# Two accumulations in two PSUM banks taken in turn, in cross-attention and in a recurrent state product

## The chip, the cores and the metric

The kernel runs on one core of a Trainium2 chip. Its time is the device time of one execution in microseconds (us); the number given for a kernel is the median of its runs. Times inside an execution come from the trace of one profiled execution.

## What is computed

A decoder layer over 16 batches of 224 rows of 512 features, in fp32, in three sublayers, each followed by a residual addition and a layer norm:

```python
x = layernorm(x + self_attention(x))              # 16 heads, causal
x = layernorm(x + cross_attention(x, ctx_1024))   # one head, 750 rows of context per batch
x = layernorm(x + ffn(x))                         # a recurrence over the 16 batches

# cross-attention
q = x @ Wq.T + bq;  k = ctx @ Wk.T + bk;  v = ctx @ Wv.T + bv
attended = softmax(q @ k.T) @ v

# ffn: c is a state [224, 512], xt is one batch [224, 512], 16 steps
ft = sigmoid(xt @ wf.T + c @ uf.T + bf)
it = sigmoid(xt @ wi.T + c @ ui.T + bi)
gt = tanh(xt @ wc.T + c @ uc.T + bc)
c  = ft * c + it * gt
h  = tanh(x @ wo.T + c_final @ uo.T + bo)
```

## The kernel before

Four stages follow one another: self-attention, cross-attention (from about 410 to 900 us of the span), the recurrence (to about 1420) and the output gate with the last norm. Each engine has its own instruction stream, written out by hand; the engines meet through semaphores, and an instruction behind a wait stays behind it. Nothing reorders the matmuls: their order is that of the Python loops in the function of TensorE.

**Split operands.** An fp32 product is made of three: each operand is split into a rounded part (hi, type fp32r) and the rest (lo), and hi x hi, lo x hi and hi x lo are added up in PSUM. KC = 4 chunks of 128 of the 512 features are contracted, XC = 6 chunks of 125 of the 750 rows of context. So an accumulation has 12 matmuls (3 products x 4 chunks) or 18 (3 x 6). Each matmul comes with its own load of the stationary operand; in the trace the loads have a row of their own (PEld), which runs ahead of the matmuls.

**Cross-attention, TensorE's turn for a batch** (function step). With T = 224 rows in TC = 2 halves of R = 112:
- p_turn turns the softmax numerators of the batch before (12 transposes, L786).
- zt (L797): the query side multiplied by a folded matrix m, 512 features out. Four results of 128 x 224 lie two to a bank in the two banks of ps_h: results 0 and 1 in the first, 2 and 3 in the second (function pair). One result is completed after the other, 12 matmuls each.
- ot (L810): context times turned weights, for the batch before. Again four results of 128 x 224, two to a bank of ps_g, 18 matmuls each, one after the other.
- s (L824): the scores, 112 rows by two halves of 376 columns. The two halves lie in two banks, and the loop over them is the innermost, with the same stationary operand for both. This one is not changed.
- x1_turn turns the next batch's rows (L778).
- out (L836): the result of ot times the value weights, for the batch before: 112 rows by 512 columns, once for each half of the rows, each in a bank of ps_h, 12 matmuls each, one half after the other.

zt waits for both residuals of the batch before last (r_done), because out leaves its results in the banks that zt writes. The residual (L989, DVE) reads a half of the rows of out once out_done says that this half is complete, and out_done is raised once for each half. DVE's stream for a batch holds, in this order at its end: the maxima of the scores, x1tl (L939, L940), the two residuals, the reciprocal of the sums. POOL's x1b (L1057) waits for the residuals as well.

**Recurrence.** c_gate makes one gate for one half of the features: two tiles of 128 x 448 in two banks of ps_gate. For each tile c_tile takes four matmuls of 448 columns (hi weights times the state's hi and lo, side by side, L1274) and then four of 224 (lo weights times the state's hi, L1276). gate_done is raised once after both tiles. There are 6 gates in each of 15 steps. Between them stands x_part (L1255): the input's share of the gates, tiles of 128 x 448 of 12 matmuls, alternating between two banks from tile to tile, not from matmul to matmul.

Of the kernel before, what the change touches and what calls it, by code (L numbers as in the profile page):

```python
# [20 lines left out]
B, T, D = 16, 224, 512  # L21
H, C = 16, 32
TC = 2
R = T // TC
KC = D // 128
TX = 750
XC, XR = 6, 125
# [7 lines left out]
def wait(eng, sem, value):  # L35

    if not (isinstance(value, int) and value <= 0):
        eng.wait_ge(sem, value)


def within(n, end):
    return not isinstance(n, int) or 0 <= n < end
# [602 lines left out]
def cross_attention(nc, io, x1, x2, raw, raw_in, shared):  # L645
# [5 lines left out]
    with ExitStack() as ctx:  # L651
        def sb(name, shape, dt=F32):
            return ctx.enter_context(nc.sbuf_tensor("x_" + name, shape, dt))

        def sem(name):
            return ctx.enter_context(nc.semaphore("x_" + name))

        identity, bv_all = shared.identity, shared.bv_all
        m_hi, m_lo, wv_hi, wv_lo = shared.m_hi, shared.m_lo, shared.wv_hi, shared.wv_lo
# [24 lines left out]
        ot_hi = sb("ot_hi", [128, KC, T], F32R)  # L684
        ot_lo = sb("ot_lo", [128, KC, T], F32R)
# [8 lines left out]
        ps_g = ctx.enter_context(nc.psum_tensor("x_ps_g", [128, 2, 512], F32))  # L694
        ps_h = ctx.enter_context(nc.psum_tensor("x_ps_h", [128, 2, 512], F32))
# [28 lines left out]
        out_done = sem("out_done")  # L724
# [10 lines left out]
        def pair(bank, k):  # L735

            return bank[:, k // 2, (k % 2) * T:(k % 2) * T + T]
# [30 lines left out]
        @block.tensor  # L768
        def _(pe):

            pe.wait_ge(pad_done, 2)

            def x1_turn(b):
                wait(pe, x1_in, 16 * (b + 1))
                wait(pe, otl_done, b - 1)
                for k in range(KC):
                    for c in range(TC):
                        mm = pe.transpose(ps_g[:, k // 2, (k % 2) * T + c * R:(k % 2) * T + c * R + R],  # L778
                                          x1_raw[:, c, 128 * k:128 * k + 128], identity[0:R, 0:R])
                mm.then_inc(x1t_done, 1)  # L780

            def p_turn(b):
                wait(pe, exp_done, TC * (b + 1))
                for j in range(XC):
                    for c in range(TC):
                        mm = pe.transpose(ps_s[0:XR, j // 2, (j % 2) * T + c * R:(j % 2) * T + c * R + R],  # L786
                                          p[:, c, XR * j:XR * j + XR], identity[0:R, 0:R])
                mm.then_inc(pt_done, 1)

            def zt(b):  # L790
                wait(pe, x1tl_done, b + 1)
                wait(pe, r_done, TC * (b - 1))
                for ck in range(KC):
                    i = 0
                    for m, x in ((m_hi, x1t_hi), (m_lo, x1t_hi), (m_hi, x1t_lo)):
                        for k in range(KC):
                            mm = pe.matmul(pair(ps_h, ck), m[:, k, 128 * ck:128 * ck + 128], x[:, k, :],  # L797
                                           start=(i == 0), stop=(i == 3 * KC - 1))
                            i += 1
                mm.then_inc(zt_done, 1)  # L800

            def ot(b):
                wait(pe, ptl_done, b + 1)
                wait(pe, cxl_done, XC * (b + 1))
                wait(pe, x1tl_done, min(b + 2, B) if isinstance(b, int) else b + 2)
                for dk in range(KC):
                    i = 0
                    for v, q in ((cx_hi, pt_hi), (cx_lo, pt_hi), (cx_hi, pt_lo)):
                        for j in range(XC):
                            mm = pe.matmul(pair(ps_g, dk), v[:, j, 128 * dk:128 * dk + 128], q[:, j, :],  # L810
                                           start=(i == 0), stop=(i == 3 * XC - 1))
                            i += 1
                mm.then_inc(ot_done, 1)

            def s(b):
                wait(pe, ztl_done, b + 1)
                wait(pe, ctl_done, KC * (b + 1))
                wait(pe, ptl_done, b)
                for c in range(TC):
                    i = 0  # L820
                    for z, x in ((zt_hi, ct_hi), (zt_hi, ct_lo), (zt_lo, ct_hi)):
                        for k in range(KC):
                            for half in range(2):
                                mm = pe.matmul(ps_s[0:R, 2 * c + half, 0:XH + 1], z[:, k, c * R:c * R + R],  # L824
                                               x[:, k, half * XH:half * XH + XH + 1], start=(i == 0), stop=(i == 3 * KC - 1))
                            i += 1
                    mm.then_inc(s_done, 1)

            def out(b):
                wait(pe, otl_done, b + 1)  # L830
                wait(pe, ztl_done, min(b + 2, B) if isinstance(b, int) else b + 2)
                for c in range(TC):
                    i = 0
                    for y, w in ((ot_hi, wv_hi), (ot_hi, wv_lo), (ot_lo, wv_hi)):
                        for k in range(KC):
                            mm = pe.matmul(ps_h[0:R, c, :], y[:, k, c * R:c * R + R], w[:, k, :],  # L836
                                           start=(i == 0), stop=(i == 3 * KC - 1))
                            i += 1
                    mm.then_inc(out_done, 1)

            def step(b):
                if within(b - 1, B):
                    p_turn(b - 1)
                if within(b, B):
                    zt(b)
                if within(b - 1, B):
                    ot(b - 1)
                if within(b, B):
                    s(b)
                if within(b + 1, B):  # L850
                    x1_turn(b + 1)
                if within(b - 1, B):
                    out(b - 1)

            x1_turn(0)
            for b in range(2):
                step(b)
            with pe.Fori(2, B - 1) as b:
                step(b)
            step(B - 1)  # L860
            step(B)
# [247 lines left out]
def recurrence(nc, io, x2, identity, cc, wf, wi, raw, raw_in):  # L1109

    GATES = ("f", "i", "c")
    HC = KC // 2
    TILES = 3 * KC
    with ExitStack() as ctx:
# [6 lines left out]
        w = {"wf": wf, "wi": wi}  # L1121
# [16 lines left out]
        ps_gate = ctx.enter_context(nc.psum_tensor("f_ps_gate", [128, 6, 512], F32))  # L1138
# [67 lines left out]
        @block.gpsimd  # L1206
        def _(pool):
            pool.memset(state[:], 0.0).then_inc(made, 1)

            def split(i):  # L1210
                _, hi, lo = plan[i]
                pool.wait_ge(raw_in[i % 3], 16 * (i // 3 + 2))
                pool.tensor_copy(hi[:], raw[i % 3][:]).then_inc(w_rounded[i], 1)  # L1213
                pool.wait_ge(w_rounded[i], 1)
                pool.tensor_tensor(lo[:], raw[i % 3][:], hi[:], ALU.subtract).then_inc(w_split[i], 1)

            split(1)
            split(4)
            pool.wait_ge(xpart_done, TILES * (B // 2))
            split(6)  # L1220
            split(7)

        @block.tensor
        def _(pe):
# [42 lines left out]
                                           start=(k == 0), stop=(k == KC - 1))  # L1267
                mm.then_inc(u_done, 1)

            def c_tile(half, j, k2, ks):  # L1270
                m = slice(128 * (HC * half + k2), 128 * (HC * half + k2) + 128)
                hi, lo = w["u" + GATES[j]]
                for k in ks:
                    pe.matmul(ps_gate[:, 2 * j + k2, 0:2 * T], hi[:, k, m], cc[:, k, :, :], start=(k == 0), stop=False, skip_group_check=True)  # L1274
                for k in ks:
                    mm = pe.matmul(ps_gate[:, 2 * j + k2, 0:T], lo[:, k, m], cc[:, k, 0, :], start=False, stop=(k == KC - 1),  # L1276
                                   skip_group_check=True)
                return mm

            def c_gate(b, half, j, ks=range(KC)):  # L1280
                if ks[0] == 0:
                    if isinstance(b, int) and b == 1 and half == 0:
                        pe.wait_ge(w_split[3 + j], 1)
                        pe.wait_ge(u_bias_done, 3)
                    wait(pe, add_done, 6 * (b - 1) + 3 * half + j - 2)
                for k2 in range(HC):
                    mm = c_tile(half, j, k2, ks)
                if ks[-1] == KC - 1:
                    mm.then_inc(gate_done, 1)

# [551 lines left out]
```

## Time and profile before

| | |
|---|---|
| median of 3 runs | 1537.86 us (1536.14 to 1540.71) |
| profiled execution | 1533.36 us |
| its span | 1531.6 us |
| mean granted TensorE clock | 0.972 |
| TensorE matmul, share of the span | 95% |
| weight loads (PEld) | 82% |
| DVE / ACT / POOL | 59% / 42% / 36% |

The span is the time from the first to the last instruction of the program in the profiled execution. A share is the time in which the engine had an instruction running; matmuls overlap, so a busy TensorE is not one at its peak. L797 is line 797 of the kernel. A clock of 1.00 is 2.4 GHz, 0.50 is 1.2 GHz.

### The profile page before, as it was taken

Reading aid. Unit: us, or ns where it says so; the run is one execution under the profiler, and the core shown is the slowest. Engines: PE = TensorE matmul, PEld = TensorE weight load, DVE = VectorE, ACT = ScalarE, POOL = GpSimd, SP = SyncE. Lnnn points to the kernel's source line nnn. Section 1 sums busy time; section 2 is a strip of 40 time slices with the busy share of each in tenths; the row PEclk is TensorE's granted clock in tenths of the full one; section 3 lists DMA queues with packets and bytes.
Section 4 is the critical chain, followed back from the end, with each engine's and each line's share of the span. In section 5 each row is a group of like instructions: output and inputs, shape, how many; then the busy total and the mean of one; then the engine's idle time right before and its main releaser. Section 6 shows DMA issues by size and latency. Waiting matters only on the chain. (4 is left out here: it accounts for less than half of the span.)

```text
span 1531.6 us, 28869 instructions
## 1 busy us (share of the span) xinstructions
PE 1455.9 (95%) x10322; PEld 1262.1 (82%) x10322; DVE 902.2 (59%) x1995; ACT 638.9 (42%) x1887; POOL 554.3 (36%) x430
## 2 busy tenths in 40 slices
PE   7999999999699999999999959999999999999897
PEld 3677777776498999999999849999999999998685
DVE  4578888887445665665665532253445435546587
ACT  4477777776243444434434313222222222221232
POOL 2445555554365656656566421000000000003254
PEclk9899999999899999999999979899999999999999
DMA  6113232243236343343334122200000000000553
GB/s 187 39 51 97 85 95 73 84 148 91 73 109 196 135 156 122 135 146 131 133 133 150 53 77 78 80 25 1 24 22 2 24 0 24 1 1 0 158 165 118
DMA packets 71605, 131.01 MB, mean 86 GB/s; under 512 B 7218, under 2 KB 15410, under 8 KB 71540
## 3 DMA queue, kind: packets, MB, share of 16 engines
q1 hardware_dynamic: 71540, 130.17, 26.6%
q8 instruction: 37, 0.61, 0.2%
q14 instruction: 28, 0.23, 0.0%
HBM read 106.30 MB, written 22.02 MB: 84 GB/s over the span
## 5 line engine op out<-in xcount | busy, mean ns | idle before, releaser
L401 ACT ACTIVATE a_p<-a_ps_s,a_nmax 112x224 f32<-112x224 f32 (+1 forms) x512 | 198.8, 417 | 96.3 <-DVE a_nmax L467 96.3
L617 POOL TENSOR_TENSOR a_p<-a_p,a_rinv 112x896 f32<-112x896 f32 (+1 forms) x128 | 164.9, 1309 | 171.8 <-DVE a_rinv L475 166.1
L1213 POOL CAST f_wf_hi<-w_raw 128x2048 fp32r<-128x2048 f32 x1 | 1.9, 1894 | 453.2 <-PE f_ps_x L1255 453.2
L1070 POOL TENSOR_TENSOR x_cx_lo<-s_cx_raw,x_cx_hi 125x512 fp32r<-125x512 f32 x96 | 120.8, 1300 | 73.1 <-ACT x_cx_hi L901 73.1
L1443 DVE TENSOR_TENSOR f_gate<-f_ps_gate,f_xg_early 128x448 f32<-128x448 f32 x45 | 28.1, 624 | 197.7 <-PE f_ps_gate L1276 197.7
L1359 ACT ACTIVATE f_gate<-f_gate 128x448 f32<-128x448 f32 x90 | 52.1, 579 | 185.3 <-DVE f_gate L1446 185.3
L1064 POOL TENSOR_TENSOR x_ct_lo<-s_ct_raw,x_ct_hi 128x750 fp32r<-128x750 f32 x64 | 118.7, 1885 | 12.6 <-ACT x_ct_hi L875 12.6
L482 DVE COPY a_pt<-a_ps_t 112x448 f32<-112x448 f32 x128 | 79.3, 620 | 64.2 <-PE a_ps_t L277 64.1
L277 PEld LDWEIGHTS a_ps_t<-identity,a_p 112*112 112x112 f32 x768 | 87.4, 135 | 33.4 <-issue 12.2
L401 ACT ACTIVATION_READ_ACCUMULATOR a_p<-a_ps_s,a_nmax 112x1 f32 x512 | 113.7, 222 | 0.0
L277 PE MATMUL a_ps_t<-identity,a_p 112*112 112x112 f32 x768 | 107.3, 262 | 0.0
L466 DVE TENSOR_REDUCE a_nmax<-a_ps_s 112x1 f32<-112x224 f32 x256 | 97.0, 379 | 12.5 <-PE a_ps_s L264 12.2
L1057 POOL TENSOR_TENSOR x_x1b<-s_x_raw,s_bv_all 112x1024 f32<-112x1024 f32 x16 | 38.1, 2380 | 88.4 <-DVE x_r L989 88.4
L467 DVE TENSOR_REDUCE a_nmax<-a_ps_s 112x1 f32<-112x112 f32 x256 | 67.4, 263 | 0.0
L977 DVE TENSOR_REDUCE x_smax<-x_ps_s 112x1 f32<-112x750 f32 x32 | 30.0, 939 | 58.5 <-PE x_ps_s L824 58.5
L309 PE MATMUL a_ps_w<-a_w_hi,a_yt_lo 128*112 128x512 f32 x128 | 64.3, 516 | 0.0
L1274 PE MATMUL f_ps_gate<-f_cc,f_uf_hi 128*128 128x448 f32 x240 | 59.8, 370 | 3.5 <-DVE f_cc L1470 3.5
L1346 ACT ACTIVATE f_xg_early<-f_ps_x,f_bias 128x448 f32<-128x448 f32 x48 | 30.4, 633 | 72.9 <-PE f_ps_x L1255 72.9
L908 ACT ACTIVATE x_p<-x_ps_s,x_shift 112x750 f32<-112x750 f32 x32 | 28.4, 888 | 75.8 <-DVE x_shift L982 75.8
L1346 ACT ACTIVATE f_xg_late<-f_ps_x,f_bias 128x448 f32<-128x448 f32 x48 | 30.4, 633 | 70.8 <-PE f_ps_x L1255 70.7
L1274 PE MATMUL f_ps_gate<-f_cc,f_ui_hi 128*128 128x448 f32 x240 | 59.8, 370 | 0.0
L1274 PE MATMUL f_ps_gate<-f_cc,f_uc_hi 128*128 128x448 f32 x240 | 59.5, 368 | 0.0
(220 smaller groups left out, 3863.6 us busy)
## 6 DMA issues: line engine op xcount, KB each, us to landing
s_ct_raw<-in_ct SPq DMA_DIRECT2D x16, 1500.0 KB, 7.9
s_cx_raw<-in_cx SPq DMA_DIRECT2D x16, 1500.0 KB
a_xt<-in_xt SPq DMA_DIRECT2D x16, 448.0 KB, 3.9
a_xrow<-in_x SPq DMA_DIRECT2D x16, 448.0 KB, 3.5
a_xres<-in_x SPq DMA_DIRECT2D x16, 448.0 KB, 4.5
x_scratch<-a_xn SPq DMA_DIRECT2D x16, 448.0 KB, 3.1
s_x_raw<-x_scratch SPq DMA_DIRECT2D x16, 448.0 KB, 3.6
x_scratch<-x_xn SPq DMA_DIRECT2D x16, 448.0 KB, 6.2
```

The costliest lines, as they stand in the source:

```text
L277: mm = pe.transpose(ps_t[0:R, (g + unit) % 2, h * R:h * R + R], src, identity[0:R, 0:R])
L309: mm = pe.matmul(ps_w[0:R, :], *products[i], start=(i == 0), stop=(i == len(products) - 1))
L401: e = act.activation((p1 if c else p0)[:, g, h, :], src, ACT.Exp, bias=nmax[:, g % 2, c, h:h + 1], accum_out=rsum[:, g % 2, c, h:h + 1])
L466: dve.tensor_reduce(nmax[:, g % 2, 1, h:h + 1], ps_s[0:R, h, 0:T], AX.X, ALU.max, negate=True)
L467: dve.tensor_reduce(nmax[:, g % 2, 0, h:h + 1], ps_s[0:R, h, T:T + R], AX.X, ALU.max, negate=True)\
L482: dve.tensor_copy(transposed(g, unit), unit_bank(g, unit)).then_inc(ptd_done, 1)
L617: pool.tensor_tensor(p[:, g, :, :], p[:, g, :, :], inv, ALU.mult).then_inc(norm_done, 1)
L1064: pool.tensor_tensor(ct_lo[:, k, 0:TX], ct_raw[:, k, :], ct_hi[:, k, 0:TX], ALU.subtract).then_inc(ctl_done, 1)
L1070: pool.tensor_tensor(cx_lo[:, j, :], cx_raw[:, j, :], cx_hi[:, j, :], ALU.subtract).then_inc(cxl_done, 1)
L1274: pe.matmul(ps_gate[:, 2 * j + k2, 0:2 * T], hi[:, k, m], cc[:, k, :, :], start=(k == 0), stop=False, skip_group_check=True)
L1346: act.activation(pre(odd_pair, half, j)[:, k2, :, :], ps_x[:, t % 2, 0:2 * T].rearrange("p (a t) -> p a t", a=2), ACT.Identity, bias=bias[ ...
L1359: act.activation(gate[:, j, cols, :], gate[:, j, cols, :], ACT.Tanh, scale=0.5 if j < 2 else 1.0).then_inc(act_done, 1)
```

## The change

Three products of cross-attention and the state product of the recurrence are put in another order. The same matmuls are done on the same operands, into the same places.

- zt and ot: results 0 and 2 (in different banks) are accumulated together, one matmul for each in turn, and then results 1 and 3.
- out: both halves of the rows are accumulated together; out_done is still raised for each half, at its last matmul, and these are now the last two.
- c_gate: the two tiles of a gate take turns; all matmuls with hi weights come first, then all with lo weights. The function c_tile is gone.

```diff
-                for ck in range(KC):
+                for first in range(KC // 2):
                     i = 0
                     for m, x in ((m_hi, x1t_hi), (m_lo, x1t_hi), (m_hi, x1t_lo)):
                         for k in range(KC):
-                            mm = pe.matmul(pair(ps_h, ck), m[:, k, 128 * ck:128 * ck + 128], x[:, k, :],
-                                           start=(i == 0), stop=(i == 3 * KC - 1))
+                            for ck in (first, first + KC // 2):
+                                mm = pe.matmul(pair(ps_h, ck), m[:, k, 128 * ck:128 * ck + 128], x[:, k, :],
+                                               start=(i == 0), stop=(i == 3 * KC - 1))
                             i += 1
...
-                for dk in range(KC):
+                for first in range(KC // 2):
...
-                            mm = pe.matmul(pair(ps_g, dk), v[:, j, 128 * dk:128 * dk + 128], q[:, j, :],
-                                           start=(i == 0), stop=(i == 3 * XC - 1))
+                            for dk in (first, first + KC // 2):
+                                mm = pe.matmul(pair(ps_g, dk), v[:, j, 128 * dk:128 * dk + 128], q[:, j, :],
+                                               start=(i == 0), stop=(i == 3 * XC - 1))
...
-                for c in range(TC):
-                    i = 0
-                    for y, w in ((ot_hi, wv_hi), (ot_hi, wv_lo), (ot_lo, wv_hi)):
-                        for k in range(KC):
+                i = 0
+                for y, w in ((ot_hi, wv_hi), (ot_hi, wv_lo), (ot_lo, wv_hi)):
+                    for k in range(KC):
+                        for c in range(TC):
                             mm = pe.matmul(ps_h[0:R, c, :], y[:, k, c * R:c * R + R], w[:, k, :],
                                            start=(i == 0), stop=(i == 3 * KC - 1))
-                            i += 1
-                    mm.then_inc(out_done, 1)
+                            if i == 3 * KC - 1:
+                                mm.then_inc(out_done, 1)
+                        i += 1
...
-                for k2 in range(HC):
-                    mm = c_tile(half, j, k2, ks)
+                hi, lo = w["u" + GATES[j]]
+                for u, columns in ((hi, 2 * T), (lo, T)):
+                    for k in ks:
+                        for k2 in range(HC):
+                            m = slice(128 * (HC * half + k2), 128 * (HC * half + k2) + 128)
+                            mm = pe.matmul(ps_gate[:, 2 * j + k2, 0:columns], u[:, k, m], cc[:, k, :, :] if u is hi else cc[:, k, 0, :],
+                                           start=(u is hi and k == 0), stop=(u is lo and k == KC - 1), skip_group_check=True)
```

## Rows read from the trace of the kernel before

**Rows 1.** The page's first part: busy us (share of the span) and instructions of each engine.
```profile
PE 1455.9 (95%) x10322; PEld 1262.1 (82%) x10322; DVE 902.2 (59%) x1995; ACT 638.9 (42%) x1887; POOL 554.3 (36%) x430
```
**Rows 2.** Windows by stage: from:to, length, busy us (instructions), PEclk, DMA share, GB/s.
```profile
550.00:960.00 410.00, 390.20 (x2702) 367.91 (x2701) 228.14 (x395) 161.62 (x306) 216.46 (x140) 0.97 0.35 117
960.00:1440.00 480.00, 470.72 (x2654) 437.38 (x2655) 221.44 (x371) 122.57 (x219) 15.68 (x7) 0.98 0.08 24
```
**Rows 3.** Windows: one period of the cross-attention loop.
```profile
550.30:579.50 29.20, 29.20 (x215) 27.80 (x214) 18.22 (x33) 12.68 (x25) 18.02 (x13) 1.00 0.42 137
```
**Rows 4.** Timeline (start us, length us, engine, line, instruction): zt and ot, first and last groups.
```profile
733.15 0.61 PE L797 MATMUL x_ps_h<-x_x1t_hi,s_m_lo 128*128 128x224 f32 x4
...
737.62 0.61 PE L797 MATMUL x_ps_h<-x_x1t_lo,s_m_hi 128*128 128x224 f32 x4
738.07 0.83 PE L810 MATMUL x_ps_g<-x_pt_hi,x_cx_hi 125*128 125x224 f32 x6
...
745.44 0.83 PE L810 MATMUL x_ps_g<-x_pt_lo,x_cx_hi 125*128 125x224 f32 x6
```
**Rows 5.** Timeline: s, second and last of its six groups of eight.
```profile
747.49 1.53 PE L824 MATMUL x_ps_s<-x_ct_lo,x_zt_hi 128*112 128x376 f32 x8
...
752.95 1.53 PE L824 MATMUL x_ps_s<-x_ct_hi,x_zt_lo 128*112 128x376 f32 x8
```
**Rows 6.** Timeline: out, second and last of its six groups of four.
```profile
756.01 1.08 PE L836 MATMUL x_ps_h<-s_wv_lo,x_ot_hi 128*112 128x512 f32 x4
...
759.71 1.09 PE L836 MATMUL x_ps_h<-s_wv_hi,x_ot_lo 128*112 128x512 f32 x4
```
**Rows 7.** Timeline: one tile of a gate, then x_part's first and last groups.
```profile
1298.54 0.99 PE L1274 MATMUL f_ps_gate<-f_cc,f_uf_hi 128*128 128x448 f32 x4
1299.36 0.60 PE L1276 MATMUL f_ps_gate<-f_cc,f_uf_lo 128*128 128x224 f32 x4
1299.80 0.99 PE L1274 MATMUL f_ps_gate<-f_cc,f_uf_hi 128*128 128x448 f32 x4
...
1306.10 0.99 PE L1255 MATMUL f_ps_x<-f_xt_hi,f_wf_hi 128*128 128x448 f32 x4
...
1320.07 0.99 PE L1255 MATMUL f_ps_x<-f_xt_lo,f_wc_hi 128*128 128x448 f32 x4
```
**Rows 8.** Timeline, all engines: from out of one batch to the next batch's zt.
```profile
729.15 0.62 DVE L940 TENSOR_TENSOR x_x1t_lo<-x_ps_g,x_x1t_hi 128x448 fp32r<-128x448 f32 x1
729.69 0.74 DVE L989 SCALAR_TENSOR_TENSOR x_r<-x_ps_h,x_rinv,x_x1b 112x512 f32<-112x512 f32 x1
...
731.60 0.75 DVE L989 SCALAR_TENSOR_TENSOR x_r<-x_ps_h,x_rinv,x_x1b 112x512 f32<-112x512 f32 x1 [1.17 <-PE x_ps_h L836]
...
732.60 0.53 PEld L797 LDWEIGHTS x_ps_h<-x_x1t_hi,s_m_hi 128*128 128x128 f32 x4
...
735.19 7.42 POOL L1064 TENSOR_TENSOR x_ct_lo<-s_ct_raw,x_ct_hi 128x750 fp32r<-128x750 f32 x4 [0.38 <-ACT x_ct_hi L875]
```
**Rows 9.** Timeline: a matmul of the recurrence that DVE releases.
```profile
1400.06 0.62 DVE L1470 SCALAR_TENSOR_TENSOR f_cc<-f_state,f_cc 128x448 fp32r<-128x448 f32 x1
...
1400.74 0.68 PE L1274 MATMUL f_ps_gate<-f_cc,f_uf_hi 128*128 128x448 f32 x2 [3.25 <-DVE f_cc L1470]
```
**Rows 10.** Timeline: from the last residual of cross-attention to the recurrence.
```profile
900.55 0.75 DVE L989 SCALAR_TENSOR_TENSOR x_r<-x_ps_h,x_rinv,x_x1b 112x512 f32<-112x512 f32 x1 [1.96 <-PE x_ps_h L836]
...
912.51 1.75 PE L1237 MATMUL f_ps_x<-identity,f_x_raw 112*128 112x112 f32 x8 [12.00 <-DMA f_x_raw<-x_scratch]
```
**Rows 11.** Windows: the start of batch 1's zt, and s of a later batch.
```profile
436.50:439.90 3.40, 3.31 (x15) 3.32 (x16) 2.43 (x6) 3.40 (x7) 1.56 (x1) 0.50 0.33 127
...
746.10:754.30 8.20, 8.20 (x50) 8.18 (x49) 3.65 (x5) 5.08 (x10) 6.34 (x6) 1.00 0.56 194
```
**Rows 12.** Timeline of TensorE: batch 1's zt and the ot behind it.
```profile
436.59 1.20 PE L797 MATMUL x_ps_h<-x_x1t_hi,s_m_hi 128*128 128x224 f32 x4 [0.50 <-DVE x_x1t_lo L940]
...
443.60 0.83 PE L810 MATMUL x_ps_g<-x_pt_hi,x_cx_hi 125*128 125x224 f32 x6
```

More of the change, by code:

```diff
@@ L1268, in u_part @@
                 mm.then_inc(u_done, 1)
[L1270 to L1278, printed above, removed]
             def c_gate(b, half, j, ks=range(KC)):
```

## The prediction

> **What bounds the kernel now.** I read the busy table first: the matmul row is busy for 95% of the span [rows 1]. Cut by stage it is 390 of 410 us in the main part of cross-attention and 471 of 480 us in the recurrence [rows 2]. One period of the cross-attention loop, 29.2 us, holds PE work from end to end at the full clock [rows 3]. The two stages that are changed are therefore bound by the rate at which TensorE starts matmuls and by nothing else; a nanosecond on each matmul is a nanosecond in the time, and a wait on TensorE has no cover.
>
> The timeline of TensorE gives that rate. A row there holds a run of matmuls; the start of a later row minus the start of an earlier one, over the matmuls between, is the spacing, which is what a matmul costs in a stream (its own duration overlaps the next).
> - zt: 737.62 - 733.15 = 4.47 us for 40 matmuls, 111.8 ns each; ot: 745.44 - 738.07 = 7.37 us for 66, 111.7 ns [rows 4]. Both are 224 columns wide, which is 93.3 ns at 2.4 GHz: some 18.4 ns more than the columns need.
> - s, which already takes two banks in turn: 752.95 - 747.49 = 5.46 us for 32, 170.6 ns; 376 columns are 156.7, so 13.9 ns more [rows 5].
> - out: 759.71 - 756.01 = 3.70 us for 16, 231.2 ns; 512 columns are 213.3, 17.9 ns more [rows 6].
> - recurrence: x_part takes 1320.07 - 1306.10 = 13.97 us for 68, 205.4 ns at 448 columns (186.7), 18.8 ns more. A state product of eight (four of 448, four of 224) takes 1.26 us, 0.82 for the wide and 0.44 for the narrow, so 205 and 110 ns [rows 7].
>
> So every product that stays in one bank pays about 18 ns beyond its columns, and the one that alternates pays 14. That is the case for the change. It is weak: s differs in three more things. Its two matmuls use the same stationary operand, they have an odd width, and their moving operand starts at an odd place; the new order has none of these (it shares the moving operand instead). And single changes of bank are already in the trace: x_part changes bank after every twelve matmuls, zt once in 48, ot once in 72, and all three show the same 18.4 to 18.8 ns. If the bank were what costs, x_part should be the cheaper one, though a saving of 4 ns in one of twelve is 0.3 ns, which the rows can't tell.
>
> **The change part by part.** The sum is made against the profiled execution (1533.36 us, span 1531.6). That one lies 4.5 us below the median of the runs, 1537.86; the difference is added to the median.
>
> (1) Order in zt and ot: 16 x 48 + 16 x 72 = 1920 matmuls of 224 columns. Nothing is added or removed, each keeps its weight load. zt_done and ot_done are still raised once, on the last matmul, so ACT and DVE are told at the same time. Bounds: all 18.4 ns saved, 35 us, at one end; the 4.5 ns that s is better by, 8.6 us, as the nearest row; at the other end I know of no reason that excludes a cost, and take 2 ns, half of that difference, +3.8 us. I take 0: the rate is the same across the bank changes that the trace has.
>
> (2) Order in out: 384 matmuls of 512 columns. Rate as in (1): 0, with 4 ns or 1.5 us as the s-like value. But here a signal moves. Before, out_done for the first half of the rows comes 12 matmuls (2.8 us) ahead of the second, and the first residual on DVE (0.74 us) lies beside the second half. Now the two come one matmul, 0.23 us, apart, both at the end. zt of the next batch waits for both residuals because it writes the same banks (r_done). In rows 8 the second residual starts at 731.60 and ends at 732.35; the weight load of zt starts at 732.60, after the twelve transposes of p_turn that stand between. From the end of a DVE instruction to the PE instruction that it releases the trace has 0.06 us (1400.06 + 0.62 to 1400.74) [rows 9], so the wait has 0.19 us to spare. Now the first residual starts at 731.60 - 0.23 = 731.37. DVE starts the next about 0.08 us ahead of the end of the one before (729.15 + 0.62 against 729.69), so the second runs from 732.04 to 732.79. That is 0.44 later; less the 0.19 to spare, TensorE stands still 0.25 us. It happens for the out of batches 0 to 13: 14 x 0.25 = **+3.5 us**. Behind the waiting matmul nothing else of use can start, as the engine's stream is in order. Bounds: 0 (if p_turn covers it after all) and 14 x 0.44 = 6.2.
> At the end of the stage the last batch has no zt, but the norm, its store and the first load of the recurrence hang on the second residual: it starts at 900.55, and TensorE starts again at 912.51 [rows 10]. **+0.4 us**.
> POOL's x1b waits for the same residuals and starts 0.44 later; its ct_lo then runs 7.4 us from 735.19, so to 742.6, and is wanted by s, which follows ot's last group of 745.44 [rows 4, 8], so nothing follows. SP's loads wait for rowbias and ct_lo, later still.
>
> (3) State product: 15 steps x 6 gates x 16 = 1440 matmuls, half of each width. Per gate, before: twice 1.26 = 2.52 us. After: eight wide, then eight narrow. Four narrow ones behind wide ones take 0.44; a longer run of narrow ones goes at the 111.8 ns of zt, so the second four take 0.447. Wide ones keep 0.82 for four. 1.64 + 0.44 + 0.447 = 2.527, so +0.007 us; x 90 = **+0.6 us**. Bounds: if all eight run at zt's rate and the wide ones at x_part's, 2.537, +1.5 us; s-like, 3.2 us saved on the wide and 2.0 on the narrow. gate_done is raised at the end of the pair as before, and both banks were already waited for together, so DVE sees no change.
>
> Sum: 3.5 + 0.4 + 0.6 = +4.5 us.
>
> **A rule that speaks against the change.** s alternates through 8.2 us and its clock is 1.00 [rows 11]. The Trainium skill, TensorE: Matmul & The Clock Gate, section "A second HAM failure mode: psum-queue depth-cycling", says that cycling through banks can leave TensorE idle so often in short stretches that its clock swings between the two levels. The trace doesn't bear it out where banks are already cycled; what it would do here is the last rival. The same page's "Back-to-back issue gap" gives N/2.4 + 2.5 ns for a warm stream; rows 4 to 7 are 11 to 16 ns above it, and an estimate from that page gives room for much more than s shows, about 15 ns x 3744 = 56 us, if the bank were the cause.
>
> **The rivals.**
> - Two banks in turn are cheaper, as in s (the other side). Spacing falls to columns + 13.9 ns: 1920 x 4.5 = 8.6, out 384 x 4.0 = 1.5, wide 720 x 4.5 = 3.2, narrow 720 x 2.8 = 2.0; 15.3 us saved. The residual's wait (+3.9) stays: -11.4, so 1526.5 us. It decides as soon as a matmul gains more than 1.2 ns on average (4.5 us over 3744). For: the 14 ns of s, in a stage with the same kinds of operand. Against: no effect of the single bank changes. Its far end, all 18 ns gone, is 1475; next to no chance.
> - The pair costs more than the run: successive weight loads now come from two places of a tile and not from the next chunk. Nothing in the trace shows it; at 2 ns, 3744 x 2 = 7.5 us more: 1550.
> - Nothing changes: the wait is covered and the rates hold: +0.6, 1538.5. Against it stands the 0.19 us of room for 0.44.
> - The clock falls. In batch 1 TensorE was at 0.50 (1.2 GHz) for 3.4 us, after it had stood idle [rows 11], and zt took 443.60 - 436.59 = 7.01 us in place of some 5.4 (48 at 111.8) [rows 12]. The new gap of 0.25 us, or the cycling, would have to bring that about once in each of 14 batches: 14 x 1.6 = 22 us, 1564.
>
> **How the numbers follow.** A measurement here can tell 0.3% (4.6 us) from no change. Forecast +4.5, with its own range 1539 to 1546: 50%. s-like gain: 27%. Pair costs more: 13%. Nothing: 7%. Clock: 3%. The forecast lies at the border, so half of it, 25%, counts as the same and half as slower. Faster: 0.25, the s-like case but for 0.02 of gains too small to tell. Same: 0.25 + 0.07 (nothing) + 0.02 + 0.02 of the dearer pair = 0.36. Slower: 0.25 + 0.11 + 0.03 = 0.39. The time is the forecast's, 1537.9 + 4.5 = 1542.4. The range takes in the s-like gain and the dearer pair, 1525 to 1551; the clock and gains beyond s are left out.
>
> **What would show it.** In the changed profile: spacing of zt, ot and out within 1 ns of 111.8, 111.7 and 231.2 (the bank does nothing); 107 in zt and ot would be the s-like rival, and then the sum is wrong by its largest term. The first residual starts 0.2 us ahead of the second's release, the second ends some 0.4 us later against the end of out, and zt's first matmul is released by DVE x_r, with an idle time of about 0.25 us, where there is none now. The period of a batch is 29.5 us in place of 29.2. A gate takes 2.52 to 2.54 us. The clock stays at 1.00 in zt and the gates.

## The result, and the profile after

| | before | after |
|---|---|---|
| median | 1536.35 us (5 runs, 1535.97 to 1540.71) | 1546.33 us (5 runs, 1543.25 to 1550.35) |
| ratio to before | 1 | 1.0058, 95% interval 1.0036 to 1.008 |
| span of the profiled execution | 1531.6 us | 1548.6 us |
| mean granted clock in it | 0.972 | 0.966 |

The change makes the kernel slower by 0.4 to 0.8%; the medians differ by 10.0 us. The profiled execution after is the slowest of its five, and the difference of the two spans, 17 us, is not the effect. Part of the rest is clock, not order. In 81 us across the start of the recurrence, where TensorE waits for loads and for DVE, the granted clock was 0.79 before and 0.76 after; the kernel after gets there 13 us later, so its window is moved by as much. From the first matmul of the state product to the last it took 502.3 us before and 505.7 after, at a clock of 0.98 and 0.97, and the third experiment, whose state product is the old one, took 506.2 us. The rows are windows: from:to, length, busy us of PE, PEld, DVE, ACT and POOL with their counts, clock, DMA share, GB/s. First before:

```profile
904.00:985.00 81.00, 70.17 (x348) 65.07 (x349) 21.65 (x28) 27.18 (x45) 15.65 (x5) 0.79 0.34 105
914.30:1416.60 502.30, 496.48 (x2808) 463.93 (x2808) 223.67 (x370) 135.41 (x235) 22.72 (x7) 0.98 0.07 24
```

and after, with a piece of 29.9 us, one period of cross-attention, ahead of it:

```profile
719.80:749.70 29.90, 29.70 (x214) 27.95 (x213) 21.18 (x33) 12.67 (x25) 17.11 (x12) 1.00 0.37 133
917.00:998.00 81.00, 70.13 (x336) 65.21 (x337) 21.33 (x28) 26.54 (x44) 15.65 (x5) 0.76 0.36 105
927.40:1433.10 505.70, 500.12 (x2808) 467.56 (x2808) 223.76 (x370) 135.19 (x235) 22.31 (x7) 0.97 0.08 23
```

The period answers to [rows 3]: TensorE was busy for all of 29.2 us, and now takes 29.9 with 0.2 of it idle; DVE's busy time went up by 3 us though its instructions are the same. The clock is 1.00 in both. Most periods are 0.70 us longer. Over all of them, from the start of zt of batch 1 to that of batch 15, it is 849.56 - 436.59 = 412.97 us before and 859.71 - 437.45 = 422.26 after, 9.3 us more, about the difference of the medians. The start before stands in [rows 12]; the end before, and then both after:

```profile
849.56 0.69 PE L797 MATMUL x_ps_h<-x_x1t_hi,s_m_hi 128*128 128x224 f32 x4
```

and

```profile
437.45 1.34 PE L798 MATMUL x_ps_h<-x_x1t_hi,s_m_hi 128*128 128x224 f32 x5 [0.49 <-DVE x_x1t_lo L943]
...
859.71 1.01 PE L798 MATMUL x_ps_h<-x_x1t_hi,s_m_hi 128*128 128x224 f32 x7
```

The timeline of TensorE after, same columns as [rows 4], out first and then zt and ot:

```profile
734.68 2.02 PE L838 MATMUL x_ps_h<-s_wv_lo,x_ot_hi 128*112 128x512 f32 x8
736.53 2.02 PE L838 MATMUL x_ps_h<-s_wv_hi,x_ot_lo 128*112 128x512 f32 x8
...
740.88 1.05 PE L798 MATMUL x_ps_h<-x_x1t_hi,s_m_lo 128*128 128x224 f32 x8
...
744.45 1.06 PE L798 MATMUL x_ps_h<-x_x1t_lo,s_m_hi 128*128 128x224 f32 x8
...
746.69 1.50 PE L812 MATMUL x_ps_g<-x_pt_hi,x_cx_lo 125*128 125x224 f32 x12
...
752.05 1.50 PE L812 MATMUL x_ps_g<-x_pt_lo,x_cx_hi 125*128 125x224 f32 x12
```

Spacing: out 1.85 us for 8, 231 ns (before 231.2 [rows 6]); zt 3.57 us for 32, 111.6 ns (111.8) and ot 5.36 us for 48, 111.7 ns (111.7) [rows 4]. And six gates of the recurrence after:

```profile
1306.33 1.79 PE L1284 MATMUL f_ps_gate<-f_cc,f_uf_hi 128*128 128x448 f32 x8
1307.96 1.05 PE L1284 MATMUL f_ps_gate<-f_cc,f_uf_lo 128*128 128x224 f32 x8
...
1321.44 0.99 PE L1258 MATMUL f_ps_x<-f_xt_hi,f_wf_hi 128*128 128x448 f32 x4
```

They take 15.11 us, 2.52 a gate, as before (1.26 a tile [rows 7]). In these rates two banks in turn bring nothing and cost nothing.

The time is lost between the products. The timeline of all engines after, from the end of out to s; it answers to [rows 8]:

```profile
738.39 1.46 PE L786 MATMUL x_ps_s<-identity,x_p 112*125 112x112 f32 x12
738.42 1.41 DVE L992 SCALAR_TENSOR_TENSOR x_r<-x_ps_h,x_rinv,x_x1b 112x512 f32<-112x512 f32 x2 [1.69 <-PE x_ps_h L838]
...
739.89 1.15 PE L798 MATMUL x_ps_h<-x_x1t_hi,s_m_hi 128*128 128x224 f32 x8
739.91 2.40 POOL L1060 TENSOR_TENSOR x_x1b<-s_x_raw,s_bv_all 112x1024 f32<-112x1024 f32 x1 [7.08 <-DVE x_r L992]
...
741.41 1.69 DVE L958 TENSOR_TENSOR x_pt_lo<-x_ps_s,x_pt_hi 125x448 fp32r<-125x448 f32 x3 [1.31 <-ACT x_pt_hi L884]
...
742.27 6.53 POOL L1067 TENSOR_TENSOR x_ct_lo<-s_ct_raw,x_ct_hi 128x750 fp32r<-128x750 f32 x4
...
743.01 6.34 DVE L949 CUSTOM_DVE_ANT_0 x_dot<-s_x_raw,s_kbias 112x512 f32<-112x512 f32 x1
...
749.39 0.69 DVE L949 CUSTOM_DVE_ANT_0 x_dot<-s_x_raw,s_kbias 112x512 f32<-112x512 f32 x1
...
751.94 1.52 DVE L965 SCALAR_TENSOR_TENSOR x_zt_lo<-x_ps_h,s_zbias,x_zt_hi 128x224 fp32r<-128x224 f32 x4
...
753.71 1.60 PE L826 MATMUL x_ps_s<-x_ct_hi,x_zt_hi 128*112 128x376 f32 x8 [0.16 <-issue]
```

Both residuals now run after out, and zt starts 0.06 us behind the second (738.42 + 1.41 = 739.83). That was forecast. From the first transpose of p_turn (L786) to zt it is 739.89 - 738.39 = 1.50 us; before, it was 1.23:

```profile
731.40 1.46 PE L786 MATMUL x_ps_s<-identity,x_p 112*125 112x112 f32 x12
...
732.63 0.69 PE L797 MATMUL x_ps_h<-x_x1t_hi,s_m_hi 128*128 128x224 f32 x4
```

The second thing was not forecast: x_dot, a product of two operands in SBUF, takes 6.34 us for the first half of the rows and 0.69 for the second. It waits out POOL's four ct_lo, which now run straight behind x1b; it ends 0.55 us behind the last of them (742.27 + 6.53 = 748.80). zt_lo is behind it in DVE's stream and ends at 753.46, and s, which could have started behind ot at 753.39 (752.05 + 12 x 111.7 ns), starts at 753.71. The view gives no releaser for this wait (issue); the experiments on x1b show that it goes when zt_lo is in time. Before, zt_lo ended at 744.27, 1.8 us ahead of s at 746.11.

### The profile page after: what moved, and what is told of

Same layout as the page of the kernel before. It is cut to its first block and busy times, and to the rows that moved or that the text cites. A ratio compares the mean times of both kernels' runs of the same rounds, so it can differ in the third digit from the quotient of the medians.

```text
span 1548.6 us, 28869 instructions
## 1 busy us (share of the span) xinstructions
PE 1468.6 (95%) x10322; PEld 1268.9 (82%) x10322; DVE 943.7 (61%) x1995; ACT 637.9 (41%) x1887; POOL 541.0 (35%) x430
## 5 line engine op out<-in xcount | busy, mean ns | idle before, releaser
L1067 POOL TENSOR_TENSOR x_ct_lo<-s_ct_raw,x_ct_hi 128x750 fp32r<-128x750 f32 x64 | 106.2, 1688 | 7.4 <-ACT x_ct_hi L878 7.4
L949 DVE CUSTOM_DVE_ANT_0 x_dot<-s_x_raw,s_kbias 112x512 f32<-112x512 f32 x32 | 105.6, 3299 | 0.6
L1444 DVE TENSOR_TENSOR f_gate<-f_ps_gate,f_gate 128x448 f32<-128x448 f32 x90 | 56.2, 625 | 3.1
L1284 PE MATMUL f_ps_gate<-f_cc,f_uf_hi 128*128 128x448 f32 x240 | 54.4, 368 | 3.2 <-DVE f_cc L1468 3.2
```

The costliest lines, as they stand in the source:

```text
L949: dve.tensor_tensor_reduce(out=dot[:], in0=x1_raw[:, c, :], in1=kbias[:], scale=1.0, scalar=0.0, op0=ALU.mult, op1=ALU.add, accum_out=rowd ...
L1067: pool.tensor_tensor(ct_lo[:, k, 0:TX], ct_raw[:, k, :], ct_hi[:, k, 0:TX], ALU.subtract).then_inc(ctl_done, 1)
L1444: dve.tensor_tensor(gate[:, j, cols, :], ps_gate[:, 2 * j:2 * j + 2, T:2 * T], gate[:, j, cols, :], ALU.add).then_inc(add_done, 1)
```

## Experiments

All times of "before" in this section are from runs on the same chip as the experiment, and each ratio is to them: a median of 1537.44 us (17 runs) for the first four below, 1537.34 (29 runs) for x1b behind rstd and the two runs behind it. "Theory A", "A2" and the like are names that the expectations give.

**Put out back, keep the rest.** The changed kernel with

```diff
-                i = 0
-                for y, w in ((ot_hi, wv_hi), (ot_hi, wv_lo), (ot_lo, wv_hi)):
-                    for k in range(KC):
-                        for c in range(TC):
+                for c in range(TC):
+                    i = 0
+                    for y, w in ((ot_hi, wv_hi), (ot_hi, wv_lo), (ot_lo, wv_hi)):
+                        for k in range(KC):
...
-                            if i == 3 * KC - 1:
-                                mm.then_inc(out_done, 1)
-                        i += 1
+                            i += 1
+                    mm.then_inc(out_done, 1)
```

> The changed kernel with out alone put back to one half of the rows after the other; zt, ot and the gates keep two accumulations in turn. Theory A (all of the loss comes from out raising its first out_done late; the order of matmuls itself costs nothing): period of a batch 29.2 us as before, first x_dot on DVE back from 6.3 us to 1.5, no idle time of TensorE ahead of zt or s, time within 2 us of before (1536.4), ratio to before 0.999 to 1.001. Theory B (taking the banks in turn in zt, ot and the gates costs something as well): 2 to 6 us above before. Theory C (two banks in turn save time and out hides it): 2 us or more below before.

1536.95 us, ratio 1.0001 (0.9987 to 1.0014). In windows, 29.2 us hold TensorE's work from end to end, as in [rows 3]:

```profile
662.00:691.20 29.20, 29.20 (x214) 27.80 (x213) 18.14 (x32) 12.64 (x26) 18.01 (x13) 1.00 0.40 134
```

The first x_dot is back at 1.52 us:

```profile
677.11 1.52 DVE L948 CUSTOM_DVE_ANT_0 x_dot<-s_x_raw,s_kbias 112x512 f32<-112x512 f32 x1
```

3360 of the 3744 matmuls still take the banks in turn, and it can't be seen in the time. Theories B and C fall, to 0.14%.

**The new order in out alone**, in the kernel before; the edit is the part of out in the change.

> The kernel before with the new order in out alone. Theory A: the whole loss is here, 9 to 11 us above before (1546), x_dot 6.3 us in 14 batches, period 29.9 us. Theory B: only part of it, 4 to 7 us above before.

1545.07 us, ratio 1.0044 (1.0031 to 1.0057): 7 us on its interval's middle, 5 to 9. That is less than Theory A's 9 to 11 and lies where Theory B's 4 to 7 ended; but a loss from the order itself, which B needs, is what the run above did not find. Theory A was also wrong on x_dot: it was kept out in 11 batches, not in 14. The profile is the best witness of the second part, since two kinds of batch stand in one execution. Here the timeline of a batch in which x_dot got in, up to its s:

```profile
679.57 7.42 POOL L1065 TENSOR_TENSOR x_ct_lo<-s_ct_raw,x_ct_hi 128x750 fp32r<-128x750 f32 x4
...
680.32 1.62 DVE L947 CUSTOM_DVE_ANT_0 x_dot<-s_x_raw,s_kbias 112x512 f32<-112x512 f32 x1
...
682.65 0.83 PE L810 MATMUL x_ps_g<-x_pt_hi,x_cx_hi 125*128 125x224 f32 x6
...
690.69 1.02 PE L824 MATMUL x_ps_s<-x_ct_hi,x_zt_hi 128*112 128x376 f32 x5
```

and the next batch, in which it did not:

```profile
709.13 6.50 POOL L1065 TENSOR_TENSOR x_ct_lo<-s_ct_raw,x_ct_hi 128x750 fp32r<-128x750 f32 x4
...
709.86 6.32 DVE L947 CUSTOM_DVE_ANT_0 x_dot<-s_x_raw,s_kbias 112x512 f32<-112x512 f32 x1
...
712.19 0.83 PE L810 MATMUL x_ps_g<-x_pt_hi,x_cx_hi 125*128 125x224 f32 x6
...
720.54 0.74 PE L824 MATMUL x_ps_s<-x_ct_hi,x_zt_hi 128*112 128x376 f32 x3
```

From ot to s: 8.04 us in the one, 8.35 in the other, and 8.04 before. The two start within 0.02 us of each other relative to POOL (0.75 and 0.73 us behind its first ct_lo). Before, the distance was 0.84 us and x_dot always got in. But the distance alone does not decide: in this run x_dot got in at 0.73, 0.73 and 0.74 us and was kept out at 0.73 in other batches. In the first batch POOL's run takes 7.42 us, in the second 6.50: what DVE loses POOL gains.

**Delay the first residual, move no matmul.** The kernel before with

```diff
-                    wait(dve, out_done, TC * b + c + 1)
+                    wait(dve, out_done, TC * (b + 1))
```

> The kernel before with no matmul moved: both residuals on DVE wait for the whole of out (the second out_done) where the first waited for its own half. Theory A says the moment of the first residual is the cause, so the loss must appear without any new order: the two residuals run after out, the second ends 0.67 us later than before, less 0.20 us of room makes 0.47 us of wait ahead of zt, and x1b on POOL follows, which pushes x_dot to 6 us and s by 0.3 us: 14 x 0.8 = 11 us above before. Theory B (order): the same time as before to 2 us, but for a wait of at most 0.1 us.

1550.26 us, ratio 1.0084 (1.0071 to 1.0097), 13 us where 11 were expected, and more than the changed kernel loses, with every matmul in its old place. In its timeline:

```profile
680.99 1.41 DVE L989 SCALAR_TENSOR_TENSOR x_r<-x_ps_h,x_rinv,x_x1b 112x512 f32<-112x512 f32 x2 [1.90 <-PE x_ps_h L836]
...
682.45 0.70 PE L797 MATMUL x_ps_h<-x_x1t_hi,s_m_hi 128*128 128x224 f32 x4 [0.27 <-DVE x_r L989]
...
685.35 6.55 DVE L946 CUSTOM_DVE_ANT_0 x_dot<-s_x_raw,s_kbias 112x512 f32<-112x512 f32 x1
```

The wait ahead of zt is there by name, and x_dot with it. The cause is when the first residual may start.

**Take x1b out of POOL's run.** The changed kernel with

```diff
-                    residual_bias(b, odd)
                     ctl(b)
+                    residual_bias(b, odd)
```

> The changed kernel with two steps of POOL exchanged: x1b behind the four ct_lo, where it stood ahead of them. The four ct_lo then no longer run straight behind x1b but as ACT's ct_hi arrive. Theory A2 (the second part of the loss, about 0.38 us a batch, is x_dot on DVE, kept out by POOL's unbroken run of SBUF work): x_dot falls below 2.5 us, s starts without a wait, the wait ahead of zt stays (0.25 us): 14 x 0.38 = 5 us less than the changed kernel, about 1541. Rival A3 (x_dot is kept out by any four ct_lo, whatever stands ahead of them): x_dot stays near 6 us and the time at 1546.

1546.88 us, ratio 1.0055 (1.0041 to 1.0068). The time is the one expected of A3. The trace says that the experiment moved the trouble and did not take it away:

```profile
684.85 1.52 DVE L949 CUSTOM_DVE_ANT_0 x_dot<-s_x_raw,s_kbias 112x512 f32<-112x512 f32 x1
...
691.40 2.39 POOL L1060 TENSOR_TENSOR x_x1b<-s_x_raw,s_bv_all 112x1024 f32<-112x1024 f32 x1
691.49 2.32 DVE L1004 TENSOR_SCALAR x_veps<-x_mv 112x2 f32<-112x2 f32 x1
693.73 1.52 DVE L965 SCALAR_TENSOR_TENSOR x_zt_lo<-x_ps_h,s_zbias,x_zt_hi 128x224 fp32r<-128x224 f32 x4
```

x_dot is back at 1.52 us, but x_veps, two elements a partition and 0.17 us before, is kept out for the whole of x1b, and zt_lo is nearly as late as ever: s starts 0.25 us later than before against ot, in place of 0.32. So this run decides nothing between A2 and A3; the next one places x1b where no such instruction of DVE stands ahead of zt_lo.

**x1b behind rstd.**

```diff
-                    residual_bias(b, odd)
                     ctl(b)
                 if within(b - 2, B):
                     power(b - 2)
                 if within(b, B):
+                    residual_bias(b, odd)
                     cxl(b)
```

> The changed kernel with POOL's x1b moved behind ct_lo and rstd of its turn. With x1b directly behind ct_lo it was x_veps on DVE, not x_dot, that took 2.3 us, and s stayed 0.26 us late. Theory A2 (s is late because a DVE instruction of the stretch ahead of zt_lo is kept out while POOL works on SBUF): now neither x_dot nor x_veps is kept out, zt_lo is in time, from ot to s 8.04 us again, period 29.55 us, 14 x 0.3 = 4 to 5 us less than the changed kernel, about 1541.5. Rival A3 (s is late for another reason, a wait on ACT or the gap ahead of zt itself): from ot to s stays at 8.3 us and the time at 1546.

1541.31 us, ratio 1.0023 (1.0009 to 1.0037); A2's figure was 1541.5.

```profile
678.74 1.15 PE L798 MATMUL x_ps_h<-x_x1t_hi,s_m_hi 128*128 128x224 f32 x8
...
681.87 1.52 DVE L949 CUSTOM_DVE_ANT_0 x_dot<-s_x_raw,s_kbias 112x512 f32<-112x512 f32 x1
...
688.50 0.17 DVE L1004 TENSOR_SCALAR x_veps<-x_mv 112x2 f32<-112x2 f32 x1
688.58 1.52 DVE L965 SCALAR_TENSOR_TENSOR x_zt_lo<-x_ps_h,s_zbias,x_zt_hi 128x224 fp32r<-128x224 f32 x4
...
690.01 2.52 DVE L1015 TENSOR_SCALAR x_xn<-x_r,x_mv,x_rstd 112x512 f32<-112x512 f32 x2
...
692.24 1.53 PE L826 MATMUL x_ps_s<-x_ct_hi,x_zt_hi 128*112 128x376 f32 x8
```

zt_lo ends at 690.10, 2.1 us ahead of s, and the wait ahead of s is gone. x_xn now pays (2.52 us for two, 0.99 before), and TensorE loses nothing by it. In all fourteen batches it is 8.04 us from ot to s, as before. From zt to s it is 13.50 us; in the kernel after, 753.71 - 739.89 = 13.82. What is left, 0.23% or 3.5 us, is the wait ahead of zt, and that is the sum that stood in the prediction for it. Theory A3 falls.

**Why does s pay 14 ns beyond its columns and the others 18?** Two runs on the reason for the change. First s with its halves one after the other, each in its own bank:

```diff
-                    i = 0
-                    for z, x in ((zt_hi, ct_hi), (zt_hi, ct_lo), (zt_lo, ct_hi)):
-                        for k in range(KC):
-                            for half in range(2):
+                    for half in range(2):
+                        i = 0
+                        for z, x in ((zt_hi, ct_hi), (zt_hi, ct_lo), (zt_lo, ct_hi)):
+                            for k in range(KC):
...
-                            i += 1
+                                i += 1
```

> The kernel before with s alone changed the other way: each of its two halves (two banks) is completed by itself, 12 matmuls in one bank, where they were taken in turn. It takes both the alternation and the shared stationary operand away and keeps width and operands. Theory W (width or operand place explains why s pays 14 ns beyond its columns and the others 18): spacing in s stays at 171 ns, time as before to 1 us. Theory S (the stationary operand loaded twice in a row, or the bank, explains it): spacing rises to 174 to 175 ns, 768 x 4 ns = 3 us above before.

1539.57 us, ratio 1.0012 (0.9994 to 1.003).

```profile
656.49 0.84 PE L824 MATMUL x_ps_s<-x_ct_lo,x_zt_hi 128*112 128x376 f32 x4
...
659.21 0.84 PE L824 MATMUL x_ps_s<-x_ct_hi,x_zt_lo 128*112 128x376 f32 x4
```

2.72 us for 16, 170.0 ns, against 170.6 with the banks in turn [rows 5]. The time could not part the theories (Theory S was 3 us), the spacing does: the low surplus of s stays without alternation and without a repeated stationary operand.

Then the repeated stationary operand in the products that pay 18 ns, in one bank:

```diff
-                    for m, x in ((m_hi, x1t_hi), (m_lo, x1t_hi), (m_hi, x1t_lo)):
-                        for k in range(KC):
+                    for k in range(KC):
+                        for m, x in ((m_hi, x1t_hi), (m_hi, x1t_lo), (m_lo, x1t_hi)):
```

and likewise in ot, out and x_part.

> The kernel before with the three products of zt, ot, out and x_part put in the order hi x hi, hi x lo, lo x hi inside each chunk, so that two matmuls in a row have the same stationary operand (hi x hi and the product with the same hi in zt, ot, out and x_part), all in one bank. Theory S (a repeated stationary operand is what makes s cheaper): spacing falls by 2 to 3 ns on average, 3072 x 2.7 = 8 us below before. Theory W: all spacings as before, time as before to 1 us.

1539.27 us, ratio 1.001 (0.9996 to 1.0023). Its zt:

```profile
677.51 0.27 PE L797 MATMUL x_ps_h<-x_x1t_lo,s_m_hi 128*128 128x224 f32 x1
...
679.63 0.27 PE L797 MATMUL x_ps_h<-x_x1t_hi,s_m_lo 128*128 128x224 f32 x1
```

19 matmuls in 2.12 us, 111.6 ns, and the time, ratio 1.001, leaves no room for the 8 us that Theory S wanted saved. Theory S falls; the width or the place of its operands is left for s, and which of the two was not tried.

## Why the prediction came out as it did

The time lies in the range and on the side forecast, at twice the forecast's size: +4.5 us forecast, 10.0 measured by the medians (0.36 to 0.8% by the ratio). That it lies in the range is luck in part: 1546.33 us is just above the forecast's own range, 1539 to 1546, and within the stated one only because that was widened to 1551 for a rival, a dearer pair, that did not come true.

- Rates of zt, ot and out, taken as unchanged: right, within 0.2 ns in each. The argument from the bank changes that the trace already has was the right one, and the case that s made for the change was no case: the two runs on s show that neither bank nor stationary operand is behind its 14 ns. The rival of a gain, at 27%, got too much for a difference that had three other explanations. The estimate of 56 us of room rests on a reading that does not hold: the Trainium skill, TensorE: Matmul & The Clock Gate, section "Back-to-back issue gap", calls N/2.4 + 2.5 ns the gap of an isolated matmul, and for a stream of weight loads and matmuls it gives 131 ns at 512 columns; this trace has 231.2 ns there, so it agrees with neither figure.
- Clock: as forecast, it stayed at 1.00 in the period.
- The state product, +0.6 us: nothing that can be seen. A run of eight narrow matmuls was expected to go at zt's pace for its second half; the wide ones made up for it (2.52 us a gate in all).
- The wait ahead of zt, 14 x 0.25 = 3.5 us: right in mechanism and size. The chain is as it was written: against the first transpose of p_turn the second residual ends 0.49 us later (0.44 forecast), 0.2 us of it is room, zt is released by DVE and starts 0.27 us later against that transpose (0.25 forecast). The last experiment on x1b, where nothing else is lost, is 0.23% above before, 3.5 us (1.4 to 5.7).
- The step that failed is the sentence on POOL: "x1b waits for the same residuals and starts 0.44 later; its ct_lo then runs 7.4 us [...] so nothing follows". The ct_lo did have its room, and ended in time. What follows is on DVE: x1b's end moved from ahead of the end of the first ct_hi to behind it, so ct_lo no longer waits for ACT, x_dot meets POOL at another moment and is kept out of all four, and zt_lo misses the end of ot. The prediction put this term at nothing. It is 0.32 us ahead of s (8.36 from ot to s in place of 8.04), and some 0.06 more in s, whose first weight load then comes straight with its first matmul: 0.38 us in each of 13 batches, 4.9 us, and little in the last (8.10 us from ot to s). From the start of out to the start of zt it is 7.14 us in place of 6.84, 0.30 more, of which 0.27 is the wait; zt itself has 0.02. 0.30 + 0.02 + 0.32 + 0.06 = 0.70 us a batch, and with less in the first two periods (0.36 and 0.41) the 9.3 us. The 0.4 us forecast for the end of the stage can't be told apart in the medians.

The rows for it stood in the trace of before. x_dot took 1.53 us there for work that takes 0.69 when POOL leaves it alone, and x_rowbias, two elements, 1.65 us in place of 0.23. The columns of mean durations show this as plain busy time. I read the cover of POOL's step and did not ask who shares something with it.

The parts add up in separate experiments: out alone 1.0044, all but out 1.0001, the changed kernel 1.0058. That out alone may lose somewhat less than the changed kernel would agree with its three batches (of 14) in which x_dot got in, 3 x 0.38 = 1.1 us; the intervals don't part the two.

Open: what decides at the end of one of POOL's instructions whether DVE gets in. With 0.84 us between the start of the first ct_lo and x_dot it always did, with the 0.44 to 0.52 of the delayed residual never, and between 0.67 and 0.75, in the changed kernel and in out alone, three times in 28, at distances at which it was kept out as well.

## What to carry to other kernels

Before a matmul order is changed, look for the signal that sits in it: finishing two accumulations together delays the first by nearly the whole length of the second (here 11 matmuls of 0.23 us, 2.5 us), and what was hidden beside the second half has to find another cover. Count the room that the consumer has, and then follow every engine that the same signal releases, also where its own deadline is far: it may keep a third one out. And where one product looks cheaper than its neighbours in one figure, list all in which it differs before giving the gain to one of them; a run that takes that one away from it costs less than the change.

## What the runs showed of the hardware

- A DVE instruction with two operands in SBUF (x_dot, 0.69 us undisturbed) took 6.3 to 6.6 us when it met four POOL instructions in a row that read and write SBUF; it ended 0.55 us behind the last of them, so it was passed over at all three boundaries between them. A DVE instruction on two elements a partition took 2.32 us in place of 0.17 behind a POOL instruction of 2.39 (x1b directly behind ct_lo). DVE instructions that read PSUM and one operand of SBUF kept their time beside POOL: pt_lo took 1.69 us for three both beside x1b and ct_lo after and mostly clear of them before, and zt_lo 1.52 us for four even where x1b started in its midst (x1b behind rstd). The Trainium skill, SBUF — State Buffer, section "Who interferes with whom", says that a DVE instruction with two SBUF inputs contends with a GpSimd instruction that reads SBUF, and that the one that comes second is blocked for the length of the other instruction. For x_dot the trace agrees; that the loser can be blocked through a whole series is more than the section says. x_veps and x_rowbias are tensor_scalar instructions with one SBUF tensor as input; the section counts such instructions among those that can contend, in a mode of their own, and no run here shows whether they ran in it.
- An fp32r matmul stream at full clock, with a weight load for each matmul, pays 18 to 19 ns beyond its columns at 224 columns (zt, ot), 448 (x_part) and 512 (out). At 224 columns it is the same in one bank (111.8 ns) and with two in turn or the stationary operand repeated (111.6), at 512 in one bank and with two in turn (231.2 both). At 376 columns it pays 13 to 14 in either order (170.0 and 170.6).
